# A two-layer graph network with experts on one core: an order of work without the spare pass, another pace of weight conversion, and the lower parts of the gathered rows shared between ScalarE and VectorE

## The reference

```python
x = x + L0_gnn(layernorm(x))     # 32 graphs of 16 nodes, 8 heads, edge bias by scatter
# block 2: top 2 of 8 experts, 512 -> 2 x 1024 -> 512, weighted sum
logits = x @ router_w + router_b
for e in range(8):
    gate, up = split(x @ Wgu[e] + bgu[e])
    acc += ((up + 1) * quick_gelu(gate) @ Wd[e] + bd[e]) * tok_w[:, e]
x = x + L1_gnn(layernorm(x))     # Chebyshev sum with five matrices, and a linear one
# block 4: top 2 of 8 experts, 512 -> 1024 -> 512
h = gelu(x @ W1[e] + b1[e]);  y += comb[:, e] * (h @ W2[e] + b2[e])
```

## Time and profile before

| | us |
|---|---|
| median of 3 runs (lowest, highest) | 704.17 (704.0, 704.88) |
| the profiled execution | 706.59 |
| its span, first to last instruction | 704.8 |
| passes of the first expert layer, first product of pass 0 to the end of pass 7's steps | 186.7 to 369.3 |
| passes of the second expert layer | 525.9 to 681.17 |

### The profile page before, as it was taken

How to read it: one execution, slowest core, us unless ns; L and a number is a source line. 1 busy time by engine, 2 the same in 40 slices (tenths; PEclk the granted TensorE clock), 3 DMA queues, 4 the chain that set the end, 5 groups by cost and what they waited for, 6 DMA issues and landing times.

```text
span 704.8 us, 20321 instructions
## 1 busy us (share of the span) xinstructions
PE 628.8 (89%) x7793; PEld 481.4 (68%) x7793; DVE 545.3 (77%) x1273; ACT 349.2 (50%) x632; POOL 115.7 (16%) x207
## 2 busy tenths in 40 slices
PE   6999999987798888889796999999979798989966
PEld 3648999954598877889693444444448697988962
DVE  6789999677899997979982795237677958788962
ACT  3542000043576777878664342112057668788851
POOL 2000000002330442232510100000014012131510
PEclk9999999999999999999995899999978899999985
DMA  9700111102188899899844810000037858788733
GB/s 299 292 2 3 48 48 47 47 3 90 46 275 324 283 332 328 322 347 300 275 138 123 342 60 1 0 1 1 0 132 273 267 177 290 226 270 304 226 99 121
DMA packets 35626, 119.16 MB, mean 169 GB/s; under 512 B 5160, under 2 KB 5752, under 8 KB 35392
## 3 DMA queue, kind: packets, MB, share of 16 engines
q1 hardware_dynamic: 30768, 112.44, 44.8%
q0 software_dynamic: 2400, 4.05, 3.8%
q10 hardware_dynamic: 2352, 1.23, 0.7%
HBM read 109.47 MB, written 8.24 MB: 167 GB/s over the span
## 4 chain that ended last, share of the span: by engine, by line
PE 55%; DVE 22%; DMA 7%; issue 7%; ACT 6%; POOL 1%; POOLq 0%; SPq 0%; ACTq 0%; DVEq 0%
DVE r_split L1151 10%; PE pb L1810 9%; PE pb L1812 9%; PE pb L1811 9%; PE pb L1940 8%; DMA r_stage<-in_chunks 7%; PE pb L2078 3%; ACT r_split L852 3%; PE pb L2111 2%; PE pb L1933 2%; PE pb L2113 2%; PE pb L2112 2%; PE pb L1934 2%; DVE r_work L1636 2%; PE pb L2128 1%
## 5 line engine op out<-in xcount | busy, mean ns | idle before, releaser
L1151 DVE SCALAR_TENSOR_TENSOR r_split<-r_stage,r_split 128x1024 f16<-128x1024 f32 (+1 forms) x144 | 210.2, 1469 | 33.5 <-ACT r_split L852 25.8
L852 ACT ACTIVATE r_split<-r_stage 128x1024 f16<-128x1024 f32 (+1 forms) x136 | 169.0, 1256 | 33.2 <-DMA r_stage<-in_chunks 19.2
L1810 PE MATMUL pb<-r_work,r_split 128*128 128x144 f16 (+9 forms) x800 | 144.9, 224 | 20.5 <-DVE r_work L1649 12.4
L1812 PE MATMUL pb<-r_work,r_split 128*128 128x144 f16 (+9 forms) x800 | 145.2, 225 | 0.0
L1811 PE MATMUL pb<-r_work,r_split 128*128 128x144 f16 (+9 forms) x800 | 145.1, 225 | 0.0
L2111 PE MATMUL pb<-r_work,r_split 128*128 128x64 f16 (+9 forms) x544 | 102.2, 228 | 21.7 <-DVE r_work L1599 12.7
L2112 PE MATMUL pb<-r_work,r_split 128*128 128x64 f16 (+9 forms) x544 | 102.5, 228 | 0.7 <-issue 0.7
L2113 PE MATMUL pb<-r_work,r_split 128*128 128x64 f16 (+9 forms) x544 | 102.5, 228 | 0.0
L1810 PEld LDWEIGHTS pb<-r_work,r_split 128*128 128x128 f16 x800 | 78.7, 99 | 27.5 <-issue 14.7
L1940 PE MATMUL pb<-r_work 128*128 128x256 f16 x512 | 84.4, 273 | 0.0
L1933 PE MATMUL pb<-r_work 128*128 128x64 f16 x512 | 83.9, 193 | 0.0
(11 more groups left out here) (321 smaller groups left out, 1202.3 us busy)
## 6 DMA issues: line engine op xcount, KB each, us to landing
r_stage<-in_chunks SPq DMA_DIRECT2D x68, 768.0 KB, 5.6
r_stage<-in_chunks SPq DMA_DIRECT2D x76, 512.0 KB, 5.5
x_dram<-x_sb SPq DMA_DIRECT2D x12, 256.0 KB, 2.7
r_gnn<-in_cheb_lin SPq DMA_DIRECT2D x3, 1024.0 KB, 8.2
r_split<-in_cheb_lin SPq DMA_DIRECT2D x3, 1024.0 KB, 13.7
x_sb<-x_dram SPq DMA_DIRECT2D x8, 256.0 KB, 3.7
x_sb<-in_x SPq DMA_DIRECT2D x4, 256.0 KB, 3.5
r_split<-in_Wq SPq DMA_DIRECT2D x1, 1024.0 KB, 8.0
```

The source lines that it names most:

```text
L852: nc.scalar.activation(x.hi(g), x.stage(g), ACT.Copy, scale=W_SCALE).then_inc(x.whi, 1)
L1151: V.scalar_tensor_tensor(x.lo(g), x.stage(g), W_SCALE, x.hi(g), ALU.mult, ALU.subtract)\
L1810: MM(o, sh, mh, start=start, stop=False)
L1812: return MM(o, sl, mh, start=False, stop=stop)
```

## The change

1. **No spare pass.** Nothing is loaded, converted or gathered for a further pass ahead of time. `find_more` now also counts the further passes and stands in step 2 of pass 1; the other list functions stand only in the branch for `n > 0`. Each engine reads `n` before the last planned pass. After it stands `If(n < 1)` with the end of the block, and `Else` with the further passes and a second copy of the end.
2. **Pace of the conversion.** `splits` is a table. In the first layer it is one chunk a step until all are done, as before. In the second layer pass 0 converts nothing in steps 0 to 2 (before: one in each of steps 0 to 4); the passes with 64 slots convert in every second step (before in the first three, in pass 6 in the first five), and passes 7 and 8 convert 6 chunks each (before 8 and 7).
3. **Matrices 4 and 3** are loaded at the end of the value projection of block 1, before chunks 4 to 7 of pass 0; matrix 1 right behind matrix 2 after the first expert layer.
4. **Lower parts.** In the first layer ACT copies `pb[4]`, `pb[5]` and `pb[6]` (`hi_parts = 3`), DVE only `pb[7]` (`lo_parts = 1`) and the slots' numbers.

The core of the diff:

```diff
-                lead = [AHEAD] * self.base if f == 0 else [3, 8, 3, 8, 3, 8, 5, 5, AHEAD]
                 self.ready_first = AHEAD if f == 0 else 6
...
+                self.hi_parts = 3 if f == 0 else 2
+                self.lo_parts = 4 - self.hi_parts
+                ahead = self.ready_first
+                if f == 0:
+                    split = [1] * (self.chunks - ahead) + [0] * ahead
+                else:
+                    wide = [2, 2, 2, 2, 2, 1, 1, 1]
+                    split = [0, 0, 0, 1, 1, 0, 1, 1, 1, 2, 2, 2, 2, 2, 1, 1, 0, 1, 0, 1, 0, 1, 0, 1] + wide + \
+                            [0, 0, 1, 0, 1, 0, 1, 0] + wide + [0, 1, 0, 1, 0, 1, 0, 1] + [1, 1, 0, 1, 1, 0, 1, 1] + \
+                            [1, 1, 1, 1, 1, 1, 0, 0]
...
+                with sp.If(n < 1):
+                    sp.wait_ge(x.y_free, x.base)
+                    reload()
+                    if f == 0:
+                        next_matrices(x.chunks)
...
+            sp.wait_ge(v_psum, T)
+            load_matrix(4)
+            load_matrix(3)
+            for c in range(AHEAD, J):
                 load_chunk(ex[0], 0, 0, c)
...
             for e in range(1, ex[0].base):
-                if e in (2, 4, 6):
-                    load_matrix({2: 4, 4: 3, 6: 1}[e])
                 load_pass(ex[0], e)
...
-                if j == 4:
+                if j == 4 and not x.final(e):
                     gathered_hi(x, e + 1, 1 - par)
...
-                for i in range(2):
+                for i in range(x.hi_parts):
+                    dst = (x.xg_hi, x.xg_lo)[i // 2][par]
                     act.wait_ge(x.xg_psum, e * 4 + (i + 1))
...
-                for i in range(2):
+                for i in range(2 - x.lo_parts, 2):
                     dve.wait_ge(x.xg_psum, e * 4 + (i + 3))
...
                 for e in range(x.base):
+                    if x.final(e):
+                        n = count_more(f, dve)
...
-                        if e == 1 and j < 5:
-                            (find_more, list_codes, list_experts, list_places, list_shares)[j](f)
-                        if e == x.base - 1 and j == 0:
-                            list_biases(f)
-                n = count_more(f, dve)
+                        if e == 1 and j == 2:
+                            find_more(f)
...
-                if j == 3:
+                if j == 3 and not x.final(e):
                     gather(x, e + 1)
...
+                with pe.If(n < 1):
+                    finish(x.base - 1)
+                with pe.Else():
+                    banks_read()
+                    gather(x, x.base)
+                    further(pe, x, n, body)
+                    finish(n + (x.base - 1))
```

More of the change, by code:

```diff
@@ L350, in build_network @@
         list_ready = sem("list_ready")
-        more_ready = sem("more_ready")
+        more_ready = [sem(f"more_ready{f}") for f in range(2)]
+        list_step = [sem(f"list_step{f}") for f in range(2)]
         rank_step = sem("rank_step")
@@ L365, in build_network @@
         moe_tables = sem("moe_tables")
-        cheb_in = [sem(f"cheb_in{m}") for m in range(K + 2)]
+        cheb_in = wraw_in + [sem(f"cheb_in{m}") for m in range(4, K + 2)]
         cheb_hi = sem("cheb_hi")
@@ L642, in more_experts @@
                 n = count_more(f, sp)
-                w = sp.value_load(list_i[f][0:1, 8:9], min_val=0, max_val=NE - 1)
-                for c in range(AHEAD):
-                    load_more(x, x.base, w, c)
                 def body(e, par):
@@ L663, in _ @@
             for e in range(1, ex[0].base):
[L664 to L665 removed]
                 load_pass(ex[0], e)
[L667 to L676 removed]
+            more_experts(0)
             for c in range(AHEAD):
@@ L687, in _ @@
                 load_pass(ex[1], e)
-            last = more_experts(1)
-            sp.wait_ge(ex[1].y_free, last + 1)
-            rows = x_dram[1][1:N + 1, :].rearrange("(t p) d -> p t d", p=P)
-            for t in range(T):
-                sp.dma_start(x_sb[:, t, :], rows[:, t, :]).then_inc(x_in[t], 16)
+            more_experts(1)
             for t in range(T):
@@ new lines, in experts @@
+                with dve.If(n < 1):
+                    finish(x.base - 1)
+                with dve.Else():
+                    list_codes(f)
+                    list_experts(f)
+                    list_places(f)
+                    list_shares(f)
+                    list_biases(f)
+                    to_slots(x, x.base)
+                    to_aux(x, x.base)
+                    for c in range(AHEAD):
+                        weight_lo(x, x.base, (c,))
+                    gathered_lo(x, x.base, x.base % 2)
+                    slots_of(x, x.base)
+                    to_slots(x, x.base + 1)
+                    to_aux(x, x.base + 1)
+                    further(dve, x, n, body)
+                    finish(n + (x.base - 1))
```

272 lines of the change are left out of this document (144 added, 128 removed).

## The result

The changed kernel takes 676.35 us (median of 4 runs, 674.2 to 677.01); the kernel before, on the same chip, 704.52 (704.0 to 710.22). The ratio is 0.958, 95% interval 0.952 to 0.963: faster, by 28 us in the medians. The forecast was 665 us, its range 650 to 679: right in sign and range, 11 us off in size. By the profiled executions it is 706.59 and 676.04 us, with spans of 704.8 and 674.3: 30.5 us gained where 39.2 were summed.

The account below looks back on a forecast made before the run. PE, DVE and the chunk stream were taken to bound the first layer's passes side by side, with list functions and jumps adding waits. Terms -11.3, -7.3, -4.7 and -15.9 sum to -39.2 us: 665 us as median, range 650 to 679.

Parts of the forecast that it names:

- Passes 0 to 6 of the first layer, -11.3: First layer: lists and matrices gone, a copy moved to ACT; passes shrink to PE's work or the stream, -11.3 us.
- Pass 7, -7.3: First layer's last pass: wait for `list_biases`, a gather and four conversions go, leaving 21.0 us, -7.3 us.
- Behind it, -4.7: After the first layer's last pass: idle 3.09 and 1.56 us go, output steps gain 1.8, jump costs 1.8; -4.7 us.
- the third rival: Clock stays full behind both last passes, halving the time of the output products: 648 to 655 us, chance 0.18.
- The price of the jump: Jump over some 700 rows between L2177 and `keep_busy`: 1.8 us taken, up to 3.1 + 1.6 possible.
- Transfers around block 3: 0.: Matrices 4 and 3 moved to the value projection cost 0; matrix 1 delaying the second layer's chunks costs 0, at worst 3 us.
- Second layer, passes 0 and 1, -6.8: Second layer: pass 0 loses PE's wait of 1.08 us, -1.2 us; pass 1 becomes like pass 5, -5.6 us.
- Passes 2 to 7, +0.7: Second layer: step-7 conversions delay wide passes 3 and 5, +0.5 us each; pass 7 has two fewer conversions, -0.3 us.
- Pass 8, -4.1: Second layer's last pass: a gather of 2.6 us and 1.3 us of waits go, leaving 15.3 us, -4.1 us.
- Behind the second layer, -5.7: After the second layer's last pass: 3.32 us of idle time goes, output steps at full clock gain 2.4; -5.7 us.
- the second rival: Jump paid in full, wide passes lose whole conversion pairs, the stream gives less: 674 to 682 us, chance 0.19.
- The last rival: ACT becomes the first layer's bound through its third copy ahead of the gelu: 700 to 710 us, chance 0.03.

Follow-up runs that it names:

- x_lists_in: Changed kernel with the five list functions again unconditional in pass 1 and the biases behind step 0 of the last pass: 690.63 us, ratio to before 0.977.
- x_mats_in: Changed kernel with matrices 4, 3 and 1 loaded again in passes 2, 4 and 6 of the first layer: 680.01 us, ratio to before 0.970.
- x_best_w: Changed kernel with old conversion places from second-layer pass 2, 14 fillers before the jump and 4 behind, loads after add-back, wide passes 3 and 5 converting 1,2,2,2,2,2,1,1: 663.39 us.
- x_fill_before: Changed kernel with 14 of the first layer's filler products ahead of the jump and 4 behind it, instead of 30 behind: 670.92 us, ratio to before 0.954.
- x_late_added: Changed kernel whose loads of matrices 2 and 1 and the second layer's first chunks wait for VectorE's add-back of the first layer's last tile: 671.39 us.
- x_pace_old: Changed kernel with the second layer's conversion table as in the kernel before: 675.08 us, ratio to before 0.960.

## Why the prediction was right, and where it was off

- **Passes 0 to 6 of the first layer, -11.3: -10.2.** The pattern of the earlier trace rows was read rightly. x_lists_in and x_mats_in put each part back and find its us. Passes 3 and 5 came out at 20.3 and 21.1, not at 23. Pass 4, for which half a microsecond less was forecast, took 1.1 more.
- **Pass 7, -7.3: -7.0.** The size was right, the split wrong: I counted the wait, the gather and the conversions apart. x_lists_in shows that `list_biases` alone is 5.5 to 6.4 us of it, wait and half clock together. That the sum came out is in part luck.
- **Behind it, -4.7: -3.1, by two errors that nearly cancel.** The idle time and the clock gave -10.9 (21.0 to 10.1 us) instead of -6.5, since the clock stayed at 1.00 up to 0.8 us before L2228's end: the third rival's mechanism, for this one place. The jump cost 7.3 us, and with the fillers behind it the transposes came 7.9 us later against L2228, instead of the 1.8 that I chose; the bounds of 1.84 and 3.09 + 1.56 did not hold it. Both rows came from quieter stretches; here SP issues 2 MB of matrices and the chunks in the same microseconds. The row of 1.84 us is also of a jump over far less code, the one loop body of `wide_scatter`, and stands eight products behind it; what the length of a jump costs, no run tells. Windows of the kernel before at its two jumps, and of the changed one at its own, show it in the DMA share (0.00 and 0.54, against 0.99):

```profile
144.00:147.00 3.00, 1.16 (x6) 0.31 (x4) 2.65 (x9) 2.20 (x6) 0.00 (x0) 1.00 0.00 0
...
369.00:373.00 4.00, 0.91 (x14) 0.74 (x12) 3.02 (x8) 0.42 (x2) 0.85 (x1) 1.00 0.54 74
```

```profile
363.00:369.00 6.00, 0.00 (x0) 0.00 (x0) 3.77 (x8) 4.64 (x9) 0.00 (x0) 0.50 0.99 307
```

  The price of the jump is the step of the sum that failed here: "on DVE and ACT the same jump lies beside PE's products" failed with it, at 2.70 us on DVE, ahead of the layer norm.
- **"Transfers around block 3: 0."** Right for the data, wrong for the instructions: with these transfers held back PE's idle time at the jump was 0.27 us (x_best_w) after 5.02 (x_fill_before). By the rule of the Trainium skill that I weighed (Runtime: NRT & Kernel Launch, Instruction fetch mechanics), a taken branch whose target is not among the instructions already fetched stalls until it is loaded. The traces agree: in each run where PE reaches the jump behind the first layer at full clock, idle time of "issue" follows, 0.27 to 7.67 us. They show besides that on PE it is longer while the DMA engines are busy: 0.27 us at a share of 0.05, 2.71 at 0.32, 3.58 to 7.67 at 0.84 and more. The profile of x_late_added lists two DMA queues of kind "instruction", 0.12 MB from 355 to 378 us; that these are what the bulk loads hold up is argued, not shown, and DVE's and ACT's jumps took as long with the loads held back.
- **Second layer, passes 0 and 1, -6.8: -7.2.** Right in sum, half for another reason. "Pass 1 becomes like pass 5" took the lists as the whole cause. They are 3.2 us (27.4 to the 24.2 of x_pace_old); 2.7 are the new table, or 1.2 by the two profiles in which pass 1 takes 23.0 us.
- **Passes 2 to 7, +0.7: +5.9.** This is the largest error, 5.2 of the 8.7 us by which the sum missed. I had the mechanism (a conversion in step 7 puts ACT behind as the wide pass begins) and priced it at half a microsecond a pass. It cost 1.5 and 1.9 us in passes 3 and 5, and 0.6, 0.5 and 1.4 in passes 2, 6 and 7. Pass 5 had its bad case here: 1.5 of the 1.9 us are PE's time at a clock of 0.93, and with the same table it took 22.1 to 23.6 us. Of pass 7's 1.4 us the old table gives back 0.4; the rest no run explains. The sum left out that every step with a pair is ACT's own 2.4 us, so that a lag at the start is kept: with 1,2,2,2,2,2,1,1 (x_best_w) both passes take 20.7 us.
- **Pass 8, -4.1: -2.5.** PE waits 2.00 us behind a conversion (L867) in step 1; the table again:

```profile
644.15 0.23 PE L1850 MATMUL pb<-r_work,r_split 128*128 128x160 f16 x1 [2.00 <-ACT r_split L867]
```

  With the old places that wait is gone, but the one for DVE's `turn_in` (L1622) is 2.13 us instead of 1.23, and the pass takes 15.6 to 16.5 us in the four runs, against 16.3 to 17.0 as changed: near the 15.3 of the sum in two of them.
- **Behind the second layer, -5.7: -6.8.** Right.

The rest of the miss is 0.9 us ahead of the expert layer, which scatters so between profiles. The forecast's own case, 656 to 673 us at 0.58, does not hold the measured 676.35; the stated range does, because it took in most of the second rival. That rival's band, 674 to 682 us at 0.19, holds the result, and two of its three terms are what happened: the jump is paid (more than in full), the pace hurts. Its third, the stream, is not: the passes gained all but 1 us. The last rival, ACT as the bound of the first layer, did not come: ACT is busy 17.0 to 17.9 us of 19.5 to 21.3 in passes 1 to 6, and PE waits there for its conversions twice, 1.38 and 0.91 us, and never for its gelu.

## What to carry to other kernels

A jump over much code in a stretch in which bulk loads start costs microseconds on the engines that take it: start the loads behind it, or put filler work ahead of it, so that nothing but the jump stands between the last product and the next data. Only the first of the two shortened the jump here, and doing both gained no more than one, since the next products then waited for the layer norm. Where a step with two conversions takes an engine as long as the step itself, a pair that stands one step too early delays every step of the pass: put the lighter steps at the change of widths, and read a table's effect pass by pass, for here a gain of 3.9 us and a loss of 5.7 hid in one sum. And vector work that nobody waits for can cost about one and a half times its length (3.9 us, 5.5 to 6.4), if it stands in the queue ahead of what PE waits for.
